# Cross-attention and FFN on one core: heads 0 to 7 of all four tiles first, then heads 8 to 15

## The chip, the core and the metric

One core of one Trainium2 chip. The metric is the device time of one execution in microseconds (us), lower is better; runs are compared by their medians.

## The reference

Eight batches; in each, 512 query rows attend to a context of 1024 rows, then a small FFN with a low-rank term follows. The mask lets through only keys that the kernel finds at run time to lie in a window of 160.

```python
# x [8,512,256], ctx [8,1024,256], 16 heads of 64
def xattn(query, key, value, mask, w_q, w_k, w_v, w_o):
    q, k, v = query @ w_q, key @ w_k, value @ w_v            # 256 -> 1024, split in 16 heads
    scores = jnp.where(mask, -jnp.inf, q @ k.T / 8)          # per head
    return (softmax(scores) @ v).merge_heads @ w_o           # 1024 -> 256
x = x + xattn(layernorm(x), ctx, ctx, mask, ...)
w = clip(round(kernel / s), -8, 7) * s                       # s = max|kernel| / 7
h = layernorm(x)
out = x + h @ w + bias + (h @ a) @ b
```

## The kernel before

**Slots.** A batch has ST = 4 tiles of 128 query rows and NG = 4 groups of 4 heads, so NS = 16 slots per batch; a slot is one tile with one group. LAST = 128 slots in all, and 12 more drain the pipeline (SLOTS, L371). Slot k is tile k % 16 // 4 and group k % 4: a tile goes through all its heads before the next one starts. u is k % 16.

**The pipeline over slots.** Five engines each run through `slot(s)` in order, held together by semaphores only.

- PE (`fast_pe`, `slot`): `scores(k+2)` (L981, 12 matmuls), `weighted_values(k-3)` (L913 with a 65-column output and L1002, 16 matmuls), then the *items* of slot k.
- DVE (`fast_dve`, `slot`, L862 on): normalises the output of slot k-4 (L868, L869), then evacuates the low half of the **first** projection item of slot k-1 (`first = 1`), then `maxima(k+1)` (L801, L805), then the rest of slot k-1's items; in slots 9 to 11 of a batch also the statistics of the layer norm for the batch three ahead (L749, `norm_var`).
- ACT (`fast_act`, `slot`): `exps(k+1)` (L671, 4 instructions), then the high halves of the items of slot k.
- POOL: `split_probs(k)` (L580 to L586) makes fp16 high and low parts of the probabilities; for some slots the per-row 1/sqrt(var) of the tail (L600 to L603).
- SP: a DMA transpose of those parts (L503), residual loads and stores of results.

The scores have two PSUM buffers: `scores(k+2)` waits for `exps(k)`.

**Items.** An item is one PSUM bank's worth of work on PE, whose result ACT rounds to fp16 (high half) and DVE subtracts (low half); matrices are multiplied as three fp16 products (`halves`, L913). Items rotate through three banks (LANES = 3, `p_item`): `claim` makes PE wait until DVE is done with the item three before. Projection items of a batch: c (context transposed), x0, x1 (normalised x transposed), k0 to k3 (keys, four heads each), q0 to q7 (queries, two heads each), v0, v1 (values, eight heads each); once in four batches h, r0, r1 (the rows 129 to 160 of four windows). Tail items of a tile: o0, o1 (attention output transposed, eight heads each), w (the product with w_o and, on DVE, the residual sum x1 and its statistics, L846 to L854), n (x2, the normalised x1, transposed), f (the FFN product and the result, L858). x2 is made on ACT (L716).

**Who is when.** PROJ lists the projection items by u; those of a batch are all made during the batch before it. Batch 0's are all made ahead of slot 0 (ALL_PROJ), and batch 1's by a denser list, FIRST_PROJ. LATE lists the tail items by k % 4, with how many tiles back: every four slots bring one n, one w, one f, one o0 and one o1, w alone in its slot. No projection items remain in batch 7.

```python
PROJ = [["c", "x0"], [], ["x1"], ["k0", "k1"], ["k2", "k3"], [], ["q0"], ["q1"],
        ["q2", "q3"], [], ["q4"], ["q5"], ["q6", "q7"], [], ["v0"], ["v1"]]
LATE = [[("n", 3)], [("w", 2)], [("f", 3), ("o0", 1)], [("o1", 1)]]
```

Of the kernel before, what the change touches and what calls it, by code (L numbers as in the profile page):

```python
# [25 lines left out]
P = 128  # L26
# [11 lines left out]
def xattn_ffn(nc, x, ctx_in, mask, w_q, w_k, w_v, w_o, kern, bias, lora_a, lora_b, out):  # L38
# [8 lines left out]
    PV_BEHIND, HALF_BUFS, TURN_BUFS = 3, 3, 4  # L47
    SCALE = DH ** -0.5
# [11 lines left out]
    with es:  # L60
# [127 lines left out]
        attn = [f.take([HD]) for _ in range(2)]  # L188
        lora_at = Layout()
        lora_at.at = f.at  # L190
        lora = lora_at.take([DT, D])
        oT_hi = f.take([HT, P], fp16)
        oT_lo = f.take([HT, P], fp16)
        x1 = f.take([D])
        x1b = [f.take([D]) for _ in range(2)]
# [150 lines left out]
        def item_evacuation(eng, kind, i, j, src, copy, scale_copy):  # L346
# [6 lines left out]
            if kind == "k":  # L353
# [31 lines left out]
        AHEAD = ["x0", "x1"] + [f"q{i}" for i in range(6)]  # L385
        ALL_PROJ = AHEAD + ["h", "c", "q6", "k0", "q7", "k1", "k2", "k3", "v0", "v1", "r0", "r1"]
        SPLIT = ("o0", "o1", "n")

        def slot_items(k):

            proj = list((FIRST_PROJ if k < NS else PROJ)[k % NS]) if k < LAST - NS else []
            if k % (NS * GROUP) // NS == 2 and k < LAST - GROUP * NS and k % NS in QUAD_ITEMS:
                proj.append(QUAD_ITEMS[k % NS])
            late = [(name, k // NG - back) for name, back in LATE[k % NG] if 0 <= k // NG - back < NT]
            return proj, late
# [8 lines left out]
        class Slot:  # L404


            def __init__(self, k):
                self.k = k
                self.u, self.batch, self.par = k % NS, k // NS, k // NS % 2
                self.t, self.g = self.u // NG, self.u % NG  # L410

                self.proj, self.late = slot_items(k)
                self.norm_ahead = k < LAST - 2 * NS
# [66 lines left out]

        def rest_ready(batch):
# [15 lines left out]
        def fast_sp(sp):  # L497
# [18 lines left out]
            def slot(s):  # L516
                if s.k < LAST:
                    turn_probs(s.k)
                if s.k == 0:
                    sp.wait_ge(keep_made, 1)  # L520
                    sp.wait_ge(zeros_made, 5)
                    rest_values(0)
                if s.u == 4 and s.batch + 1 < B:
                    rest_values(s.batch + 1)
                if s.u == (4 if s.batch == 0 else 1) and s.norm_ahead:

                    sp.wait_ge(xn_made, ST * (s.batch + 2))
                    sp.dma_start(x_in, x_v[s.batch + 2]).then_inc(x_loaded, 16)
                tile = s.k // NG - 1
# [5 lines left out]
                tile = s.k // NG - 3  # L535
                if s.g == 3 and 0 <= tile:
                    sp.wait_ge(out_made, tile + 1)
                    sp.dma_start(outt_v[tile], y[:, tile % 2]).then_inc(out_stored[tile % 2], 16)
# [20 lines left out]
        def fast_pool(pool):  # L559
# [34 lines left out]
            def slot(s):  # L594
                if s.k < LAST:
                    split_probs(s.k)
                tile = s.k // NG - 2
                if s.g == 2 and 0 <= tile < NT:
# [4 lines left out]
                    nc.gpsimd.tensor_tensor(x1b[tile % 2], x1, bias_all[:, :], ALU.add).then_inc(x1b_made, 1)  # L603
                if s.u == 1 and s.norm_ahead:
                    pool.wait_ge(item_made, ALL_PROJ.index("c") + 1 if s.batch == 0 else items_at[s.k - 1 - NS] + 1)
# [18 lines left out]
        def fast_act(act):  # L624

            def item(s, i, name):

                par = 1 - s.par
# [52 lines left out]
            def tail_item(s, i, name):  # L681
# [4 lines left out]
                else:  # L686
                    m = slice(HT // 2 * int(name[1]), HT // 2 * (int(name[1]) + 1))
                    ins = nc.scalar.activation(oT_hi[:, m, :].rearrange("p t q -> p (t q)"), bank[:, :], ACT.Copy)  # L688
# [3 lines left out]
            for i, name in enumerate(ALL_PROJ):  # L692
# [11 lines left out]
                if name == "k3":  # L704
                    exps(1)
                if name in ("v1", "r1"):
# [5 lines left out]
            def slot(s):  # L712
                for name, tile in s.late:
                    if name == "n":
                        act.wait_ge(t_rstd_made, tile + 1)
                        nc.scalar.activation(x2, x1, ACT.Identity, bias=t_shift[:, :], scale=t_rstd[:, :]) \  # L716
                            .then_inc(x2_made, 1)
# [7 lines left out]
                for i, (name, _) in enumerate(s.late):  # L725
                    if name in SPLIT:
                        tail_item(s, len(s.proj) + i, name)
# [6 lines left out]
        def fast_dve(dve):  # L734
# [26 lines left out]
            def item(s, i, name):  # L761

                par = 1 - s.par
# [43 lines left out]
            for i, name in enumerate(ALL_PROJ):  # L807
# [3 lines left out]
                if name == "k1":  # L811
                    maxima(0)
                if name == "k2":
                    maxima(1)
                if name == "v0":
                    maxima(2)
                if name == "r0":
                    maxima(3)
# [6 lines left out]
            def tail_item(s, i, name, tile):  # L825
# [7 lines left out]
                if name[0] == "o":  # L833
                    m = slice(HT // 2 * int(name[1]), HT // 2 * (int(name[1]) + 1))
                    nc.vector.tensor_tensor(oT_lo[:, m, :].rearrange("p t q -> p (t q)"), bank[:, :],  # L835
                                            oT_hi[:, m, :].rearrange("p t q -> p (t q)"), ALU.subtract) \
# [4 lines left out]
                elif name == "w":  # L841

                    dve.wait_ge(res_loaded[tile % 2], 16 * (tile // 2 + 1))
                    if tile >= 1:
                        dve.wait_ge(x1b_made, tile)
                    nc.vector.scalar_tensor_tensor(out=x1, in0=bank[:, 0:D], scalar=1.0 / (WS * WS),  # L846
# [8 lines left out]
                else:  # L855
                    dve.wait_ge(x1b_made, tile + 1)
                    dve.wait_ge(out_stored[tile % 2], 16 * (tile // 2 + 1))
                    nc.vector.tensor_tensor(y[:, tile % 2], bank[:, 0:D], x1b[tile % 2], ALU.add).then_inc(out_made, 1)  # L858
# [3 lines left out]
            def slot(s):  # L862
                k = s.k - PV_BEHIND - 1
                if 0 <= k < LAST:
# [5 lines left out]
                        attn[k // NG % 2][:, k % NG * GROUP * DH:(k % NG + 1) * GROUP * DH]  # L870
# [32 lines left out]
        def fast_pe(pe):  # L903
# [18 lines left out]
            def item(s, i, name):  # L922

                kind, j = name[0], int(name[1:] or 0)
                bank = claim(s, i)
                if kind == "c":
# [31 lines left out]
            def queries_done(batch, grp):  # L958

                last = f"q{2 * grp + 1}"  # L960
                if batch == 0:
                    return max(ALL_PROJ.index(last), ALL_PROJ.index(f"k{grp}")) + 1
                k = next(k for k in range((batch - 1) * NS, batch * NS) if last in slot_items(k)[0])
                return Slot(k).item(slot_items(k)[0].index(last), 1)

            def scores(k):

                par, t, grp = k // NS % 2, k % NS // NG, k % NG
# [18 lines left out]
            def weighted_values(k):  # L987

                par, grp = k // NS % 2, k % NG
# [16 lines left out]
            for i, name in enumerate(ALL_PROJ):  # L1006
# [7 lines left out]
                if name == "k1":  # L1014
                    scores(0)
                if name == "k2":
                    scores(1)
                if name == "v0":
                    scores(2)
                if name == "r0":  # L1020
                    scores(3)
# [3 lines left out]
            def tail_item(s, i, name, tile):  # L1025

                bank = claim(s, i)
                if name[0] == "o":

                    pe.wait_ge(attn_made, NG * tile + (2 if name == "o0" else 4))  # L1030
                    for m in range(HT // 2):
                        c = int(name[1]) * HT // 2 + m
                        mm = nc.tensor.transpose(bank[:, m * P:(m + 1) * P],  # L1033
                                                 attn[tile % 2][:, c * P:(c + 1) * P], ident[:, :])
                elif name == "w":
                    if tile == 0:
                        pe.wait_ge(split_lo[3], 1)
                    pe.wait_ge(item_done, items_at[s.k - 1])
                    mm = halves(bank[:, 0:D], [(oT_hi[:, m, :], oT_lo[:, m, :], wt(3, 0)[:, m, :],
                                                wt(3, 1)[:, m, :]) for m in range(HT)])  # L1040
# [581 lines left out]
```

## Time and profile before

| | us |
|---|---|
| median of 3 runs | 501.69 (500.94 to 502.58) |
| the profiled execution | 500.28 |
| its span, first to last instruction | 497.3 |

The profiled execution lies 3.0 us over its span (what comes before and after the instructions) and 1.4 us under the median. Busy shares of the span are PE 90%, PE weight loads 65%, DVE 81%, ACT 66%, POOL 80%. Such shares are a mean over stretches with different limits, so the views to read are the busy time by batch and the chain of waits within a few slots.

### The profile page before, as it was taken

To read this page: it belongs to the slowest core of one execution; us is meant where nothing else is said; L and a number is where in the kernel's file an instruction comes from. 1 tells how busy PE (TensorE), PEld (TensorE's weight loads), DVE (VectorE), ACT (ScalarE), POOL (GpSimd) and SP (SyncE) were. 2 spreads that over 40 slices of the span, in tenths; PEclk is the share of its full clock that TensorE was granted. 3 is DMA by queue.
4 is the path that set the end of the run, shared out by engine and by line. 5 is a ranking of instruction groups with operands and counts; after the bars stand their busy time and mean duration, and the time that the engine had idled before them with its cause. 6 is when DMAs were issued, how large, how long until landed. Compare 5 with 4: busy or idle time off the path is not lost.

```text
span 497.3 us, 15466 instructions
## 1 busy us (share of the span) xinstructions
PE 448.2 (90%) x5855; PEld 325.1 (65%) x5855; DVE 403.5 (81%) x1110; ACT 327.2 (66%) x845; POOL 398.4 (80%) x659
## 2 busy tenths in 40 slices
PE   3878789999999999999999999999999999888874
PEld 1335556787766866777666866687667876676652
DVE  4876779987988989788988989888988888878662
ACT  4967566875677766776677766776677666656530
POOL 5786578999788977789788978898787977899941
PEclk9789999999999999999999999999999999999897
DMA  8602585797857996789866985799776976779950
GB/s 292 206 23 43 117 192 111 137 201 160 160 115 144 190 153 118 119 181 162 147 125 134 195 160 119 148 171 168 137 132 126 163 153 122 146 139 173 150 127 27
DMA packets 218818, 71.91 MB, mean 145 GB/s; under 512 B 202786, under 2 KB 216883, under 8 KB 218739
## 3 DMA queue, kind: packets, MB, share of 16 engines
q1 hardware_dynamic: 217680, 69.25, 72.7%
q0 software_dynamic: 480, 1.31, 1.0%
q8 instruction: 49, 0.80, 0.7%
q10 hardware_dynamic: 578, 0.30, 0.2%
q14 instruction: 31, 0.25, 0.2%
HBM read 14.71 MB, written 4.19 MB: 38 GB/s over the span
## 4 chain that ended last, share of the span: by engine, by line
PE 42%; DVE 25%; ACT 17%; POOL 8%; issue 4%; DMA 2%; SPq 0%; DVEq 0%; POOLq 0%; ACTq 0%
PE ps_b L913 32%; ACT arena L671 8%; DVE ps_a L801 8%; PE ps_a L981 6%; DVE arena L794 4%; DVE arena L783 2%; ACT arena L650 2%; POOL arena L584 2%; POOL arena L580 2%; DMA arena<-in_L_xattn_w_q_dram 2%; DVE arena L869 2%; ACT arena L662 2%; PE ps_b L1033 2%; ACT arena L622 1%; DVE arena L805 1%
## 5 line engine op out<-in xcount | busy, mean ns | idle before, releaser
L913 PE MATMUL ps_b<-arena 128*128 128x65 f16 (+3 forms) x3348 | 321.6, 248 | 8.3 <-DVE arena L869 4.2
L913 PEld LDWEIGHTS ps_b<-arena 128*128 128x128 f16 x3348 | 222.5, 98 | 84.1 <-issue 7.9
L671 ACT ACTIVATE arena<-ps_a,arena 128x160 f32<-128x160 f32 x512 | 159.9, 395 | 93.5 <-DVE arena L805 84.9
L584 POOL TENSOR_TENSOR arena<-arena 128x512 f16<-128x512 f32 x128 | 148.1, 1157 | 0.0
L580 POOL CAST arena<-arena 128x512 f16<-128x512 f32 x128 | 78.2, 611 | 54.3 <-ACT arena L671 53.3
L801 DVE TENSOR_REDUCE ps_a<-ps_a 128x4 f32<-128x640 f32 x128 | 105.3, 823 | 0.0
L981 PE MATMUL ps_a<-arena 64*128 64x160 f16 x1536 | 75.8, 231 | 13.2 <-ACT arena L671 13.2
L981 PEld LDWEIGHTS ps_a<-arena 64*128 64x128 f16 x1536 | 50.5, 94 | 38.1 <-issue 20.6
L1002 PE MATMUL ps_b<-arena 128*128 128x65 f16 x512 | 71.4, 193 | 0.0
L869 DVE TENSOR_TENSOR arena<-ps_b,arena 128x256 f32<-128x256 f32 x128 | 54.3, 424 | 4.4
L794 DVE TENSOR_TENSOR arena<-ps_b,arena 128x512 f16<-128x512 f32 x60 | 41.1, 687 | 20.2 <-ACT arena L662 18.9
L688 ACT ACTIVATE arena<-ps_b 128x512 f16<-128x512 f32 x64 | 38.4, 602 | 25.6 <-PE ps_b L1033 25.6
L586 POOL TENSOR_TENSOR arena<-arena 128x128 f16<-128x128 f32 x128 | 54.8, 428 | 0.0
L581 POOL CAST arena<-arena 128x256 f16<-128x256 f32 x128 | 51.2, 400 | 0.0
L1002 PEld LDWEIGHTS ps_b<-arena 128*128 128x128 f16 x512 | 50.1, 98 | 0.0
L835 DVE TENSOR_TENSOR arena<-ps_b,arena 128x512 f16<-128x512 f32 x64 | 43.8, 686 | 5.8 <-DVE mask_u L858 1.0
L662 ACT ACTIVATE arena<-ps_b 128x512 f16<-128x512 f32 x58 | 34.9, 604 | 17.7 <-PE ps_b L913 16.5
L1033 PE MATMUL ps_b<-ident,arena 128*128 128x128 f32 x256 | 38.4, 273 | 0.1
L1033 PEld LDWEIGHTS ps_b<-ident,arena 128*128 128x128 f32 x256 | 30.2, 141 | 4.8 <-DVE arena L835 0.2
L600 POOL TENSOR_TENSOR arena<-arena,neg_half 128x1 f32<-128x1 f32 x32 | 17.7, 552 | 17.4 <-DVE arena L854 17.1
L805 DVE TENSOR_SCALAR arena<-ps_a 128x4 f32<-128x4 f32 x128 | 20.7, 162 | 4.4
L868 DVE RECIPROCAL arena<-ps_b 128x4 f32<-128x4 f32 x128 | 22.2, 174 | 2.5 <-PE ps_b L1002 2.1
(139 smaller groups left out, 418.8 us busy)
## 6 DMA issues: line engine op xcount, KB each, us to landing
arena<-in_x_dram SPq DMA_DIRECT2D x8, 512.0 KB
mask_u<-in_x_dram SPq DMA_DIRECT2D x32, 128.0 KB, 2.9
out_dram<-mask_u SPq DMA_DIRECT2D x32, 128.0 KB, 2.6
arena<-arena SPq DMA_TRANSPOSE x128, 4.0
arena<-arena SPq DMA_DIRECT2D x24, 65.0 KB, 2.6
arena<-in_L_xattn_w_q_dram SPq DMA_DIRECT2D x1, 1024.0 KB, 8.7
arena<-in_L_xattn_w_k_dram SPq DMA_DIRECT2D x1, 1024.0 KB, 10.7
arena<-in_L_xattn_w_v_dram SPq DMA_DIRECT2D x1, 1024.0 KB, 12.3
```

What stands on the lines that cost most here:

```text
L580: nc.gpsimd.tensor_copy(hi_main, main).then_inc(p_hi_made, 1)
L581: nc.gpsimd.tensor_copy(rests[:, :, 0:2, :], rest.unsqueeze(2).broadcast_to([P, GROUP, 2, REST])) \
L584: nc.gpsimd.tensor_tensor(lo_main, main, hi_main, ALU.subtract)
L586: nc.gpsimd.tensor_tensor(rests[:, :, 2, :], rest, rests[:, :, 0, :], ALU.subtract).then_inc(p_lo_made, 1)
L671: ins = nc.scalar.activation(probs[k % 2][:, h, :], p_scores[k % 2][:, h % 2, h // 2 * WINDOW:(h // 2 + 1) * WINDOW], ACT.Exp, bias=neg_ma ...
L794: ins = nc.vector.tensor_tensor(f_q[par][:, 1, j, :], bank[:, :], f_q[par][:, 0, j, :], ALU.subtract)
L801: link(nc.vector.tensor_reduce(p_max[k % 2].rearrange("p (i e) -> p e i", e=2), p_scores[k % 2][:, :, 0:2 * WINDOW].rearrange("p e (i k) - ...
L869: nc.vector.tensor_tensor(attn[k // NG % 2][:, k % NG * GROUP * DH:(k % NG + 1) * GROUP * DH] .rearrange("p (h d) -> p h d", h=GROUP), out ...
L913: mm = nc.tensor.matmul(dst, a, c, start=(first and at == 0), stop=(last and at == n - 1))
L981: mm = nc.tensor.matmul(p_scores[k % 2][:, e, i * WINDOW:(i + 1) * WINDOW], f_q[par][own, q_half, m, t * P:(t + 1) * P], f_k[par][own, k_h ...
L1002: mm = nc.tensor.matmul(dst, turn[:, 2, e, :], vr[par][:, h, :], start=False, stop=True)
L1033: mm = nc.tensor.transpose(bank[:, m * P:(m + 1) * P], attn[tile % 2][:, c * P:(c + 1) * P], ident[:, :])
```

## The change

Slot k is now half k % 16 // 8, tile k % 8 // 2 and group 2 * half + k % 2: the four tiles go through heads 0 to 7 in slots 0 to 7, and through heads 8 to 15 in slots 8 to 15. What the second half needs (q4 to q7, k2, k3, v1: OWN) is made in slots 0 to 7 of its own batch; the rest for the next batch is made in slots 6 to 14. So q6, q7, k2, k3 and v1 of batch 0 leave the start, and batch 7 gets seven projection items. Tiles end at slots 9, 11, 13 and 15, so the tail items come every two slots in a part of the batch: tile t's o0 at slot 5 + 2t, its o1 at 13 + 2t, w at 15 + 2t, n at 18 + 2t, f at 20 + 2t (counted on into the next batch). By u the items are now:

| u | items | u | items |
|---|---|---|---|
| 0 | q4 q5 k2 | 8 | x1 n f |
| 1 | w o1 | 9 | c q0 o0 |
| 2 | q6 q7 n | 10 | k0 k1 f |
| 3 | w o1 | 11 | q1 o0 |
| 4 | k3 n f | 12 | q2 (h) |
| 5 | w o0 | 13 | q3 (r0) o1 |
| 6 | x0 n f | 14 | v0 (r1) |
| 7 | v1 o0 | 15 | w o1 |

DVE's w now waits for the x2 of the tile before (`x2_made`), and ACT makes x2 at the end of its slot, one slot ahead of n, instead of at the beginning of n's slot. Each item's own instructions, the scores, the values and their counts stay. The core of the diff (buffers: half-size `attn`, `oT_hi`/`oT_lo` with a part per tile for the first half, three `x1b`):

```diff
-        PROJ = [["c", "x0"], [], ["x1"], ["k0", "k1"],
-                ["k2", "k3"], [], ["q0"], ["q1"],
-                ["q2", "q3"], [], ["q4"], ["q5"],
-                ["q6", "q7"], [], ["v0"], ["v1"]]
-        QUAD_ITEMS = {5: "h", 7: "r0", 11: "r1"}
-        FIRST_PROJ = [["c", "x0"], ["x1"], ["k0", "k1"], ["k2"],
-                      ["k3", "q0"], ["q1"], ["q2"], ["q3", "q4"],
-                      ["q5"], [], ["q6"], ["q7", "v0"],
-                      ["v1"], [], [], []]
+        PROJ = [["q4", "q5", "k2"], [], ["q6", "q7"], [],
+                ["k3"], [], ["x0"], ["v1"],
+                ["x1"], ["c", "q0"], ["k0", "k1"], ["q1"],
+                ["q2"], ["q3"], ["v0"], []]
+        OWN = ("q4", "q5", "q6", "q7", "k2", "k3", "v1")
+        QUAD_ITEMS = {12: "h", 13: "r0", 14: "r1"}
-        LATE = [[("n", 3)], [("w", 2)], [("f", 3), ("o0", 1)], [("o1", 1)]]
+        HALF = NS // 2
+        GH = NG // 2
+        LATE = [("w", 6), ("o1", 4), ("o0", 4 - HALF), ("f", 11), ("n", 9)]
-        ALL_PROJ = AHEAD + ["h", "c", "q6", "k0", "q7", "k1", "k2", "k3", "v0", "v1", "r0", "r1"]
+        ALL_PROJ = AHEAD + ["h", "c", "k0", "k1", "v0", "r0", "r1"]
+        def place(k):
+            half, rest = divmod(k % NS, HALF)
+            return half, rest // GH, half * GH + rest % GH
+        def tile_at(k, after):
+            rest = k - after - (HALF + GH - 1)
+            if rest < 0 or rest % GH or rest % NS >= HALF or rest // NS >= B:
+                return None
+            return rest // NS * ST + rest % NS // GH
         def slot_items(k):
-            proj = list((FIRST_PROJ if k < NS else PROJ)[k % NS]) if k < LAST - NS else []
+            proj = [name for name in PROJ[k % NS] if (k < LAST - NS if name not in OWN else
+                                                      k < LAST and (k >= NS or name not in ALL_PROJ))]
...
-                tile = s.k // NG - 2
-                if s.g == 2 and 0 <= tile < NT:
+                tile = tile_at(s.k, 7)
+                if tile is not None:
                     pool.wait_ge(t_var_made, tile + 1)
...
             def slot(s):
-                for name, tile in s.late:
-                    if name == "n":
-                        act.wait_ge(t_rstd_made, tile + 1)
-                        nc.scalar.activation(x2, x1, ACT.Identity, bias=t_shift[:, :], scale=t_rstd[:, :]) \
-                            .then_inc(x2_made, 1)
                 if DEEP - 1 <= s.k < LAST - 1:
                     exps(s.k + 1)
...
+                tile = tile_at(s.k, 8)
+                if tile is not None:
+                    act.wait_ge(t_rstd_made, tile + 1)
+                    nc.scalar.activation(x2, x1, ACT.Identity, bias=t_shift[:, :], scale=t_rstd[:, :]) \
+                        .then_inc(x2_made, 1)
...
                     if tile >= 1:
                         dve.wait_ge(x1b_made, tile)
+                        dve.wait_ge(x2_made, tile)
...
+                if s.k >= 0 and name in ("q0", "k0"):
+                    pe.wait_ge(item_done, made_at("x1" if name == "q0" else "c", s.batch + 1))
```

## Rows read from the trace of the kernel before

**Rows 1.** Busy time by stretch (us, us busy, clock): batches 0, 2, 4, 7.
```profile
51.76:97.70 45.94, 40.84 (x565) 28.48 (x565) 40.04 (x106) 29.99 (x83) 34.44 (x59) 1.00 0.71 143
...
152.88:210.42 57.54, 56.19 (x742) 41.02 (x742) 49.31 (x136) 39.82 (x107) 46.77 (x80) 1.00 0.81 145
...
265.37:320.16 54.79, 53.22 (x727) 39.66 (x727) 47.44 (x133) 38.19 (x104) 46.71 (x80) 1.00 0.81 152
...
429.49:474.30 44.81, 36.51 (x584) 29.79 (x584) 35.49 (x102) 26.57 (x77) 41.58 (x72) 0.96 0.93 159
```

**Rows 2.** PE by time in batch 4 (start, us, what): u = 1 to 3.
```profile
268.95 0.59 PE L981 MATMUL ps_a<-arena 64*128 64x160 f16 x12 [0.34 <-ACT arena L671]
...
269.97 2.78 PE L913 MATMUL ps_b<-arena 128*128 128x256 f16 x24
272.68 0.59 PE L981 MATMUL ps_a<-arena 64*128 64x160 f16 x12
...
273.70 0.63 PE L939 MATMUL ps_b<-ident,arena 128*128 128x128 f32 x4
274.17 0.82 PE L913 MATMUL ps_b<-arena 128*128 128x256 f16 x6
274.82 0.60 PE L1033 MATMUL ps_b<-ident,arena 128*128 128x128 f32 x4
...
276.37 1.82 PE L913 MATMUL ps_b<-arena 128*128 128x160 f16 x24
```

**Rows 3.** PE by time, batch 0: two query items.
```profile
70.07 2.75 PE L913 MATMUL ps_b<-arena 128*128 128x512 f16 x12
```

**Rows 4.** The chain of waits in batch 0 (start, us, what).
```profile
71.18 1.25 ACT arena L671 x4
72.43 0.50 ACT arena L662
...
72.95 0.69 DVE arena L794
73.64 0.75 DVE ps_a L801
...
74.42 0.17 DVE arena L805
...
74.61 1.26 ACT arena L671 x4
```

**Rows 5.** ACT by time in batch 4: the exponentials of u = 0 to 4, an x2.
```profile
267.56 1.25 ACT L671 ACTIVATE arena<-ps_a,arena 128x160 f32<-128x160 f32 x4 [0.29 <-DVE arena L805]
...
270.79 1.25 ACT L671 ACTIVATE arena<-ps_a,arena 128x160 f32<-128x160 f32 x4 [0.67 <-DVE arena L805]
273.21 1.25 ACT L671 ACTIVATE arena<-ps_a,arena 128x160 f32<-128x160 f32 x4 [1.16 <-DVE arena L805]
...
276.66 1.25 ACT L671 ACTIVATE arena<-ps_a,arena 128x160 f32<-128x160 f32 x4 [0.60 <-DVE arena L805]
...
279.16 0.59 ACT L716 ACTIVATE arena<-arena 128x256 f32<-128x256 f32 x1
279.75 1.25 ACT L671 ACTIVATE arena<-ps_a,arena 128x160 f32<-128x160 f32 x4
```

**Rows 6.** DVE by time in batch 4: item w, and a pair of norm statistics.
```profile
273.13 0.42 DVE L846 SCALAR_TENSOR_TENSOR arena<-ps_b,mask_u 128x256 f32<-128x256 f32 x1
...
274.40 0.17 DVE L868 RECIPROCAL arena<-ps_b 128x4 f32<-128x4 f32 x1
...
297.83 0.74 DVE L749 BATCH_NORM_STATS2 arena<-arena 128x6 f32<-128x256 f32 x2
```

**Rows 7.** The start by time: ACT's exponentials of slot 4.
```profile
56.85 1.25 ACT L671 ACTIVATE arena<-ps_a,arena 128x160 f32<-128x160 f32 x4 [0.43 <-DVE arena L805]
```

**Rows 8.** The end by time: POOL's last two splits, PE's last w (24) and f (6).
```profile
469.10 0.62 POOL L580 CAST arena<-arena 128x512 f16<-128x512 f32 x1
...
474.30 0.61 POOL L580 CAST arena<-arena 128x512 f16<-128x512 f32 x1
...
476.33 0.43 POOL L586 TENSOR_TENSOR arena<-arena 128x128 f16<-128x128 f32 x1
...
484.34 3.44 PE L913 MATMUL ps_b<-arena 128*128 128x256 f16 x30
```

More of the change, by code:

```diff
@@ L187, in xattn_ffn @@
         raw_w = [raw_q, raw_k, raw_v, f_raw.take([DT * HD])]
-        attn = [f.take([HD]) for _ in range(2)]
         lora_at = Layout()
-        lora_at.at = f.at
+        lora_at.at = f.at + HT * D
+        attn = [f.take([HD // 2]) for _ in range(2)]
         lora = lora_at.take([DT, D])
-        oT_hi = f.take([HT, P], fp16)
-        oT_lo = f.take([HT, P], fp16)
+        oT_hi = f.take([ST + 1, HT // 2, P], fp16)
+        oT_lo = f.take([ST + 1, HT // 2, P], fp16)
         x1 = f.take([D])
-        x1b = [f.take([D]) for _ in range(2)]
+        x1b = [f.take([D]) for _ in range(X1B_BUFS)]
         x2 = f.take([D])
@@ L392, in slot_items @@
             if k % (NS * GROUP) // NS == 2 and k < LAST - GROUP * NS and k % NS in QUAD_ITEMS:
                 proj.append(QUAD_ITEMS[k % NS])
-            late = [(name, k // NG - back) for name, back in LATE[k % NG] if 0 <= k // NG - back < NT]
+            late = [(name, tile_at(k, after)) for name, after in LATE if tile_at(k, after) is not None]
             return proj, late
@@ L477, in ffn_weights, with made_at @@
             nc.vector.tensor_tensor(ffn_w[:, :, :], ffn_t[:, :, :], lora, ALU.add).then_inc(ffn_made, 1)
+        def made_at(name, batch):
+            if batch == 0 and name in ALL_PROJ:
+                return ALL_PROJ.index(name) + 1
+            u = next(u for u in range(NS) if name in PROJ[u])
+            k = (batch if name in OWN else batch - 1) * NS + u
+            return items_at[k] + slot_items(k)[0].index(name) + 1
         def rest_ready(batch):
@@ L534, in slot @@
                     sp.dma_start(x_res[:, tile % 2], xt_v[tile]).then_inc(res_loaded[tile % 2], 16)
-                tile = s.k // NG - 3
-                if s.g == 3 and 0 <= tile:
+                tile = tile_at(s.k, 12)
+                if tile is not None:
                     sp.wait_ge(out_made, tile + 1)
@@ L596, in slot @@
                     split_probs(s.k)
-                tile = s.k // NG - 2
-                if s.g == 2 and 0 <= tile < NT:
+                tile = tile_at(s.k, 7)
+                if tile is not None:
                     pool.wait_ge(t_var_made, tile + 1)
@@ L626, in item @@
             def item(s, i, name):
-                par = 1 - s.par
+                par = s.par if name in OWN and s.k >= 0 else 1 - s.par
                 kind, j = name[0], int(name[1:] or 0)
@@ L686, in tail_item @@
                 else:
-                    m = slice(HT // 2 * int(name[1]), HT // 2 * (int(name[1]) + 1))
-                    ins = nc.scalar.activation(oT_hi[:, m, :].rearrange("p t q -> p (t q)"), bank[:, :], ACT.Copy)
+                    part = tile % ST if name == "o0" else ST
+                    ins = nc.scalar.activation(oT_hi[:, part].rearrange("p t q -> p (t q)"), bank[:, :], ACT.Copy)
                 ins.then_inc(item_hi, 1)
@@ L724, in slot @@
                     item(s, i, name)
-                for i, (name, _) in enumerate(s.late):
+                for i, (name, tile) in enumerate(s.late):
                     if name in SPLIT:
-                        tail_item(s, len(s.proj) + i, name)
+                        tail_item(s, len(s.proj) + i, name, tile)
+                tile = tile_at(s.k, 8)
+                if tile is not None:
+                    act.wait_ge(t_rstd_made, tile + 1)
+                    nc.scalar.activation(x2, x1, ACT.Identity, bias=t_shift[:, :], scale=t_rstd[:, :]) \
+                        .then_inc(x2_made, 1)
                 if s.norm_ahead and s.u >= NS - ST:
@@ L761, in item @@
             def item(s, i, name):
-                par = 1 - s.par
+                par = s.par if name in OWN and s.k >= 0 else 1 - s.par
                 kind, j = name[0], int(name[1:] or 0)
@@ L833, in tail_item @@
                 if name[0] == "o":
-                    m = slice(HT // 2 * int(name[1]), HT // 2 * (int(name[1]) + 1))
-                    nc.vector.tensor_tensor(oT_lo[:, m, :].rearrange("p t q -> p (t q)"), bank[:, :],
-                                            oT_hi[:, m, :].rearrange("p t q -> p (t q)"), ALU.subtract) \
+                    part = tile % ST if name == "o0" else ST
+                    nc.vector.tensor_tensor(oT_lo[:, part].rearrange("p t q -> p (t q)"), bank[:, :],
+                                            oT_hi[:, part].rearrange("p t q -> p (t q)"), ALU.subtract) \
                         .then_inc(item_done, 1)
@@ L857, in tail_item @@
                     dve.wait_ge(out_stored[tile % 2], 16 * (tile // 2 + 1))
-                    nc.vector.tensor_tensor(y[:, tile % 2], bank[:, 0:D], x1b[tile % 2], ALU.add).then_inc(out_made, 1)
+                    nc.vector.tensor_tensor(y[:, tile % 2], bank[:, 0:D], x1b[tile % X1B_BUFS], ALU.add).then_inc(out_made, 1)
                     dve.wait_ge(out_made, tile + 1)
@@ L925, in item @@
                 bank = claim(s, i)
+                if s.k >= 0 and name in ("q0", "k0"):
+                    pe.wait_ge(item_done, made_at("x1" if name == "q0" else "c", s.batch + 1))
+                if s.k >= 0 and name == "r0":
+                    pe.wait_ge(item_done, rest_ready(s.batch + 2))
                 if kind == "c":
@@ L958, in queries_done @@
             def queries_done(batch, grp):
[L960 to L964, printed above, removed]
+                return max(made_at(name, batch) for name in (f"q{2 * grp}", f"q{2 * grp + 1}", f"k{grp}"))
             def scores(k):
-                par, t, grp = k // NS % 2, k % NS // NG, k % NG
+                par = k // NS % 2
+                _, t, grp = place(k)
                 if t == 0:
@@ L987, in weighted_values @@
             def weighted_values(k):
-                par, grp = k // NS % 2, k % NG
+                par = k // NS % 2
+                half, t, grp = place(k)
+                if k % HALF == 0:
+                    pe.wait_ge(item_done, made_at(f"v{half}", k // NS))
                 pe.wait_ge(turned[k % TURN_BUFS], 16 * (k // TURN_BUFS + 1))
@@ L1013, in fast_pe @@
                 item(start, i, name)
[L1014 to L1021, printed above, removed]
+                if name in ("k1", "v0", "r0", "r1"):
+                    scores(("k1", "v0", "r0", "r1").index(name))
             pe.wait_ge(keep_made, 1)
@@ L1038, in tail_item @@
                     pe.wait_ge(item_done, items_at[s.k - 1])
-                    mm = halves(bank[:, 0:D], [(oT_hi[:, m, :], oT_lo[:, m, :], wt(3, 0)[:, m, :],
-                                                wt(3, 1)[:, m, :]) for m in range(HT)])
+                    mm = halves(bank[:, 0:D], [(oT_hi[:, part, m], oT_lo[:, part, m], wt(3, 0)[:, c + m, :],
+                                                wt(3, 1)[:, c + m, :])
+                                               for part, c in ((tile % ST, 0), (ST, HT // 2)) for m in range(HT // 2)])
                 elif name == "n":
```

32 lines of the change are left out of this document (13 added, 19 removed).

## The prediction

> **What bounds the kernel now.** I read the busy time by batch first. In a steady batch (batch 4) PE is busy 53.2 of 54.8 us and DVE 47.4, POOL 46.7; batch 2, which carries h, r0 and r1, takes 57.5; batch 0 takes 45.9 for its last 14 slots with PE busy 89% of it, and batch 7, which makes no projections, 44.8 with PE at 81% and POOL at 93% [rows 1]. So the body is filled by PE, and the two ends are not. Batches 1 to 6 run from 97.70 to 429.49, 331.8 us in all.
>
> The second view is PE by time, for the price of an item on PE, from one start to the next. A slot's scores and values take 1.02 (268.95 to 269.97), w 2.71 (269.97 to 272.68), an x of four transposes 0.47, f 0.65, and an o about as much as an x, 0.53; a busy time is 0.16 longer than the step to the next one, so two k are 1.66 and two q 2.59 [rows 2, 3]. v has the form of q, 1.30; n and c are half an x, 0.3. By these prices a batch is 16 x 1.02 and 36.4 of items, 52.8 us.
>
> The third view is the one that decides here, the chain of waits where PE does not fill the time [rows 4]. The exponentials of a slot start at 71.18, those of the next at 74.61, and between them stand, one after the other: exponentials 1.25, ACT's high half of the slot's first projection item 0.5, DVE's low half 0.69, the maximum 0.75 and its scaling 0.17. That is **3.43 us per slot, however little PE has to do**, because DVE evacuates the first projection item ahead of the next maximum, ACT puts the item's high half behind its exponentials, and scores(k+2) waits for exps(k). ACT's starts in batch 4 show the same ring by kind of item: 3.23 after a c (267.56 to 270.79), 2.42 in a slot without a projection item, 3.45 after an x, 3.09 after a k [rows 5]. In the kernel before it rarely stops PE, since projection slots (3.43 at most) alternate with w slots, where PE needs 3.73 and the ring 2.42 or less.
>
> **The change, part by part.** It adds no matmul. It moves items, and so the question is which slots get shorter than the ring.
>
> *Heavy slots, u = 15 and 0 to 5.* Four of w and o at 1.02 + 2.71 + 0.53 = 4.26; q4 q5 k2 4.45; q6 q7 n 3.92; k3 n f 2.80. Together 28.2 us, all PE's, as the ring needs at most 3.43 here.
>
> *Light slots, u = 6 to 14.* Each has a projection item first, nine in a row. PE's work is 9 x 1.02 + 15.4 = 24.6 us. The ring from the exponentials of slot 6 to those of slot 14 needs 3 x 3.43 for x0, v1 and x1, 3.23 for c, 3.09 for k0 and 3 x 3.43 for q1 to q3, 26.9. Before it, the exponentials of slot 6 come 1.1 after PE enters the slot: ACT must first make the o0 of slot 5 and the x2 that is now behind it, each about 0.6 [rows 5], less an overlap. After it, scores follow exponentials by 1.3 to 1.4 (267.56 to 268.95) [rows 2, 5]. So slots 6 to 14 take 1.1 + 26.9 + 1.3 = 29.3 instead of 24.6. A batch is 28.2 + 29.3 = 57.5.
>
> *Waits that are new in this order.* In slots 4 and 6 there are three items behind a [w, o] slot, and f needs the bank of that o. DVE's w now waits for the x2 before it, which stands on ACT behind the o: about 1.2 into the slot, then w for 1.27 (273.13 to 274.40), then o for 0.6: f can start at 3.1, and PE's work before it is 2.15 in slot 4, so +0.9 there [rows 6]. In slot 6 the same delay goes into the ring, because DVE reaches x0 late: +0.8. In slots 9 to 11 DVE does norm statistics (0.74 a pair) [rows 6] beside two or three items per slot: its own work from one maximum to the next is then 3.4, 3.8 and 3.6 by the durations above, against 3.2, 3.1 and 3.4 of the ring, +1.1. Queued behind these waits on DVE are the next maximum, behind it ACT's exponentials and PE's scores. I take all three, 2.8, so a batch is **60.2 us**; with none of them 57.5, and below that only as rival 2 has it. POOL has 46.7 per batch [rows 1] and its tail work every second slot falls where slots last 4.3, so I cost it at nothing; if that cover were gone the bound is its wait for w's statistics, again DVE's.
>
> *Batches 1 to 6.* Five at 60.2; batch 6, which prepares no norm, 59.1; and h, r0, r1 in slots 12 to 14, where PE waits anyway, cost 1.0 instead of the 2.7 of before (57.5 against 54.8) [rows 1]. 361.1 against 331.8: +29.3.
>
> *The start.* q6, q7, k2, k3 and v1 leave it: 3 x 1.30 + 2 x 0.83 = 5.6 us of PE, on the path, since the start is one chain through PE, ACT and DVE. The exponentials of slot 4 stood at 56.85 [rows 7]; I walk them to 52. From there slots 4 and 5 and DVE's FFN preparation are 9.2, the ring from 6 to 14 26.9 and 0.7 for the statistics, then 1.3 and slot 15 with 4.26: batch 1 starts at 94.4 instead of 97.70, **-3.3**. Batch 0 gives back 2.3 of the 5.6, since its light slots are bound by the ring too.
>
> *The end.* Batch 7 begins with the same heavy slots, now with its own q4 to q7, k2, k3: 24.8 us for slots 0 to 5 (28.2 less slot 15, and the 0.9 of slot 4). By the same walk POOL is done with the last of four tails 4.1 later; it then has nine splits at 2.4 (474.30 to 476.76) [rows 8] with 0.7 lost at v1: its last split ends 51.1 after the batch's start, before 476.7 - 429.5 = 47.2, +3.9. Behind it three w instead of two still lie around and after the last values: one more w in line (2.7), the new wait of w for x2 and the o behind it (1.8), and 0.7 of waiting for the x2 of tile 28. The last w ended 57.6 after the batch's start (484.34 + 2.7) [rows 8], now 66.7; what follows it is unchanged. **+9.1** with the 3.9.
>
> Sum: -3.3 + 29.3 + 9.1 = +35.1 on a span of 497.3, that is 532.4, and 535.4 for the profiled execution of 500.28. Against the median of 501.69, 1.4 higher, it is **536.8 us**.
>
> The Trainium skill, "Perfetto Trace Analysis", section "Optimization Strategy", says that a kernel whose limiting engine changes over time may gain from interleaving those regimes. This change does the reverse inside a batch: w slots and projection slots alternated and now stand in two blocks. The rule gives no figure, and the sum above does without it.
>
> **The rivals.**
>
> *1. The ring is hidden, and PE's work alone counts.* Then a batch is 52.8 instead of 54.8 to 55.3, since the stall of slot 0 (265.37 to 268.95, 3.58 against 2.1 of work) [rows 1, 2] goes too: 6 x -2.4 = -14, -3.3 to -5.6 at the start, +5 at the end for eight more us of PE in a batch with about 8 us of PE idle: 488 us. For it: PE is busy 97% of a batch. Against it: 3.43 in rows 4 with PE waiting. 6%.
>
> *2. The ring holds, but the boundary swallows most of it.* If the exponentials of slot 6 come 1.0 before PE enters the slot, as is possible once ACT is not held by o and x2, the light slots 6 to 14 are 27.2 and a batch 55.4, as before. What is left is -3.3 and +5: 503; with half of the difference 515. Against it: the o is PE's last item of slot 5, so ACT cannot be early. 14%, of which 3% lie within 0.3% of before.
>
> *3. Slower, and more: the clock falls in the light slots.* PE would be idle 20% of slots 6 to 14. Batch 7 had PE at 81% and a granted clock of 0.96, batch 0 89% and 1.00 [rows 1]. At 1.2 GHz for slots 12 to 14 their 7.4 us of PE work become 14.8, against 10.3 of the ring, +4.5 in each of seven batches: 536.8 + 31 = 568. 7%. The Trainium skill, "TensorE: Matmul & The Clock Gate", section "A second HAM failure mode: psum-queue depth-cycling", describes a kernel whose short idle times between matmul groups that cycle through PSUM banks made the clock swing; by that rule this rival would be the likely one, and batch 7, with much the same idle share at 0.96, speaks against it.
>
> *The forecast*, ring and DVE waits as walked, 522 to 550: 73%.
>
> **How the numbers follow.** The time is the forecast's, 536.8. Its own range is from no new waits (57.5 per batch: 6 x -2.7 = -16, 521) to 1.5 us more per batch and 4 at the end (550). The range for 8 in 10 adds the upper half of rival 2: 512 to 552. A difference of 0.3%, 1.5 us, is about what a measurement of this kernel can tell from none. Faster: rival 1 and a part of 2, 0.07; same: 0.03; slower: 0.90.
>
> **What would show it.** In the profile after: PE's busy share in batches 1 to 6 falls from 97% to about 88%; PE's scores wait for ACT's exponentials in u = 7 to 15; exponentials stand 3.4 us apart in u = 6 to 14 while slots 15, 1, 3 and 5 take 4.3; DVE's w waits for x2; batch 1 starts near 94; the last split of POOL ends some 51 us after batch 7 began. Wrong would be: exponentials closer than 3.2 in the light slots (the ring is not a ring), a batch under 57 (rival 2), a clock under 0.97 in the body (rival 3), or a start that gains nothing.

## The result

The changed kernel takes **548.65 us** (median of 4 runs, 544.81 to 550.84) against 502.01 (4 runs) for the kernel before: ratio 1.0934, 95% interval 1.0878 to 1.0991. It is slower, by 46.6 us; forecast were 536.8 and 512 to 552. The profiled execution took 544.81 with a span of 543.0. One of the four runs of e6 below is in the chip's slower state (553.47 at a granted clock of 0.944), so its time is given as the median of the other three.

Busy time by batch, changed kernel, as rows 1 had it for the kernel before (stretch, its length, then us busy of PE, PE's weight loads, DVE, ACT and POOL, granted clock): the last 14 slots of batch 0, batches 1, 4 and 6, batch 7 up to the end of POOL's last split, the end.

```profile
48.42:99.00 50.58, 38.61 (x519) 26.52 (x520) 39.02 (x96) 30.67 (x85) 36.42 (x61) 0.93 0.75 136
...
99.00:159.39 60.39, 54.31 (x728) 39.61 (x728) 47.30 (x133) 37.68 (x103) 47.93 (x81) 1.00 0.76 140
...
281.32:341.71 60.39, 54.30 (x727) 39.59 (x727) 47.38 (x133) 37.68 (x103) 46.84 (x80) 1.00 0.72 138
...
402.10:462.10 60.00, 54.24 (x727) 39.59 (x727) 45.58 (x122) 36.33 (x100) 44.68 (x77) 1.00 0.70 128
462.10:513.20 51.10, 43.07 (x625) 32.81 (x625) 37.84 (x107) 29.53 (x83) 43.51 (x75) 0.97 0.78 138
513.20:543.00 29.80, 16.69 (x177) 13.88 (x174) 11.52 (x41) 5.50 (x11) 5.81 (x13) 0.95 0.22 56
```

A steady batch is 60.39 us instead of 54.79 [rows 1], with the same instructions on every engine: DVE is busy for 47.4, POOL for 46.8. PE was busy 97% of a batch and is now busy 90%. The chain of waits through slots 5 to 8 of batch 4 (start, us, what) says why (whole lines are left out at the dots):

```profile
302.98 2.62 PE ps_b L927 x24
305.60 0.45 PE ps_b L1045 x4
...
306.57 0.60 ACT arena L745
...
307.29 0.44 DVE arena L860
307.75 0.43 DVE arena L864
...
308.64 0.60 DVE arena L848
309.24 0.10 DVE arena L882
309.37 0.42 DVE arena L883
309.79 0.60 DVE arena L793
310.39 0.75 DVE ps_a L820
311.16 0.17 DVE arena L824
311.36 1.25 ACT arena L690 x4
312.61 0.59 ACT arena L669
313.22 0.75 DVE arena L802
313.98 0.75 DVE ps_a L820
314.75 0.17 DVE arena L824
314.94 1.12 ACT arena L690 x4
```

Read it downwards: PE's w and o of slot 5 end the heavy stretch (L927, L1045). ACT makes x2 behind the o (L745). DVE's w waits for that x2 (L860); then come its o (L848), the output of an older slot (L882, L883), x0's low half (L793) and the maximum (L820). From 311.36 on it is the ring of the prediction, that is, the closed round of waits from one slot's exponentials to the next slot's: exponentials, v1's high half (L669) and low half (L802), maximum, exponentials at 314.94, 3.58 later. PE is in none of the lines after 306. The waits by sum over the whole execution (who waited for whom: us in all, times, longest) show the same two places. The second line did not exist before, and PE's wait for the exponentials grew from 13.2 to 30.7 us:

```profile
ACT arena L690 <- DVE arena L824: 96.5, 88, 2.4
...
DVE arena L860 <- ACT arena L745: 48.0, 23, 3.7
PE ps_a L996 <- ACT arena L690: 30.7, 39, 2.9
```

### The profile page after: what moved, and what is told of

The parts are those of the page before. It is cut to its first block, busy times and chain, and to the rows that moved or that the text cites. A ratio compares the mean times of both kernels' runs of the same rounds, so it can differ in the third digit from the quotient of the medians.

```text
span 543.0 us, 15520 instructions
## 1 busy us (share of the span) xinstructions
PE 454.8 (84%) x5855; PEld 326.7 (60%) x5855; DVE 405.4 (75%) x1110; ACT 324.6 (60%) x845; POOL 399.3 (74%) x659
## 4 chain that ended last, share of the span: by engine, by line
PE 40%; DVE 36%; ACT 15%; issue 5%; DMA 2%; POOL 1%; SPq 0%; DVEq 0%
PE ps_b L927 31%; ACT arena L690 9%; DVE ps_a L820 8%; PE ps_a L996 5%; DVE arena L813 3%; DVE arena L848 3%; PE ps_b L1045 3%; DVE arena L883 2%; ACT arena L745 2%; DVE arena L824 2%; DVE arena L793 2%; DVE arena L860 1%; DVE arena L864 1%; DVE arena L768 1%; ACT arena L681 1%
## 5 line engine op out<-in xcount | busy, mean ns | idle before, releaser
L927 PE MATMUL ps_b<-arena 128*128 128x65 f16 (+3 forms) x3348 | 326.2, 249 | 22.2 <-DVE arena L883 5.7
L927 PEld LDWEIGHTS ps_b<-arena 128*128 128x128 f16 x3348 | 223.4, 98 | 97.9 <-issue 11.4
L820 DVE TENSOR_REDUCE ps_a<-ps_a 128x4 f32<-128x640 f32 x128 | 105.3, 823 | 0.0
L996 PE MATMUL ps_a<-arena 64*128 64x160 f16 x1536 | 76.2, 232 | 31.4 <-ACT arena L690 30.7
L996 PEld LDWEIGHTS ps_a<-arena 64*128 64x128 f16 x1536 | 51.0, 95 | 59.9 <-ACT arena L690 29.8
L883 DVE TENSOR_TENSOR arena<-ps_b,arena 128x256 f32<-128x256 f32 x128 | 54.3, 424 | 4.4
L860 DVE SCALAR_TENSOR_TENSOR arena<-ps_b,mask_u 128x256 f32<-128x256 f32 x32 | 13.6, 424 | 54.6 <-ACT arena L745 48.0
L848 DVE TENSOR_TENSOR arena<-ps_b,arena 128x512 f16<-128x512 f32 x64 | 43.6, 681 | 0.0
L1045 PE MATMUL ps_b<-ident,arena 128*128 128x128 f32 x256 | 38.5, 273 | 0.0
L1045 PEld LDWEIGHTS ps_b<-ident,arena 128*128 128x128 f32 x256 | 30.7, 141 | 5.9 <-DVEq L874 0.9
L882 DVE RECIPROCAL arena<-ps_b 128x4 f32<-128x4 f32 x128 | 22.2, 174 | 4.8 <-PE ps_b L1020 4.3
```

The source lines that it names most:

```text
L820: link(nc.vector.tensor_reduce(p_max[k % 2].rearrange("p (i e) -> p e i", e=2), p_scores[k % 2][:, :, 0:2 * WINDOW].rearrange("p e (i k) - ...
L848: nc.vector.tensor_tensor(oT_lo[:, part].rearrange("p t q -> p (t q)"), bank[:, :], oT_hi[:, part].rearrange("p t q -> p (t q)"), ALU.subt ...
L883: nc.vector.tensor_tensor(attn[k // GH % 2][:, k % GH * GROUP * DH:(k % GH + 1) * GROUP * DH] .rearrange("p (h d) -> p h d", h=GROUP), out ...
L927: mm = nc.tensor.matmul(dst, a, c, start=(first and at == 0), stop=(last and at == n - 1))
L996: mm = nc.tensor.matmul(p_scores[k % 2][:, e, i * WINDOW:(i + 1) * WINDOW], f_q[par][own, q_half, m, t * P:(t + 1) * P], f_k[par][own, k_h ...
L1045: mm = nc.tensor.transpose(bank[:, m * P:(m + 1) * P], attn[pair % 2][:, m * P:(m + 1) * P], ident[:, :])
```

## The experiments

**e1 to e4: the two causes, one at a time and together.** e1 and e2 turn DVE's order in the changed kernel and in the kernel before:

```diff
-                first = 1        # low half of the slot's first projection item, then maxima
+                first = 0        # maxima first
```

e3 makes x2 on ACT earlier, behind the exponentials of its slot and ahead of the slot's high halves; e4 is both on the changed kernel.

```diff
                 if DEEP - 1 <= s.k < LAST - 1:
                     exps(s.k + 1)
+                tile = tile_at(s.k, 8)
+                if tile is not None:
+                    act.wait_ge(t_rstd_made, tile + 1)
+                    nc.scalar.activation(x2, x1, ACT.Identity, bias=t_shift[:, :], scale=t_rstd[:, :]) \
+                        .then_inc(x2_made, 1)
...
                         tail_item(s, len(s.proj) + i, name, tile)
-                tile = tile_at(s.k, 8)
-                if tile is not None:
-                    act.wait_ge(t_rstd_made, tile + 1)
-                    nc.scalar.activation(x2, x1, ACT.Identity, bias=t_shift[:, :], scale=t_rstd[:, :]) \
-                        .then_inc(x2_made, 1)
```

> The changed kernel with DVE's order turned: the maximum of a slot ahead of the first projection item, so that the item's high and low half leave the ring of exponentials, high half, low half, maximum. Theory (the ring sets slots 6 to 14): exponentials no longer stand 3.4 us apart there, slots 11 to 14 shrink to PE's 2.4 to 2.9, a steady batch falls from 60.4 to 55 to 57 us, and the whole to about 515 us. Rival (banks, DVE's load or the DMA transposes hold the light slots): a batch stays within 1 us of 60.4 and the time within 1% of 548.65.

> The kernel before with the same turn of DVE's order. Theory: the ring binds here only in batch 0 (14 slots in 45.9 us) and in the slot behind v1 (3.58 instead of 2.1), so batch 0 falls by 2 to 4 us, a steady batch from 54.8 to 53 to 54, and the whole to 490 to 495 us. Rival (the order of maxima matters nowhere): 501.7 within 0.3%.

> The changed kernel with x2 made on ACT right behind the exponentials of its slot instead of behind the high halves of that slot's items, so that DVE's w doesn't wait for the o that PE makes after it. Theory: slot 4 loses 0.9, slot 6 1.2, the exponentials behind w slots come 0.5 earlier, and a steady batch is 2 to 3 us shorter (57.5 to 58.4); the whole about 530 us, 3 of it at the end. Rival (DVE's wait for x2 costs nothing, since the ring follows anyway): a batch stays within 0.5 us of 60.4.

> The changed kernel with both edits: maximum ahead of the first projection item, and x2 right behind the exponentials. Theory: what is left is PE's work, 52.8 us a batch, plus waits for banks; a batch of 53 to 55, the whole 497 to 507 us. Rival (a third cause in the new order, such as POOL or the DMA transposes): a batch over 57.

Measured, beside 499.9 us for the kernel before on the same chip (13 runs):

| | median us | ratio, 95% interval | steady batch us |
|---|---|---|---|
| e1 maximum first | 527.47 | 1.0556 (1.0503 to 1.0608) | 57.88 |
| e3 x2 early | 530.38 | 1.0612 (1.0575 to 1.0649) | 58.63 |
| e4 both | 497.99 | 0.9951 (0.9921 to 0.9980) | 54.36 |
| e2 maximum first, kernel before | 489.91 | 0.9817 (0.9796 to 0.9838) | 53.76 |

The rows of batch 4 in e1, e2, e3 and e4 (columns as above):

```profile
270.76:328.64 57.88, 54.70 (x727) 39.92 (x727) 47.31 (x133) 37.83 (x103) 46.51 (x80) 1.00 0.81 147
```
```profile
259.25:313.01 53.76, 52.99 (x727) 39.62 (x727) 47.37 (x133) 37.61 (x104) 46.70 (x80) 1.00 0.83 155
```
```profile
275.06:333.69 58.63, 53.84 (x728) 39.71 (x728) 47.69 (x133) 37.79 (x103) 46.97 (x80) 1.00 0.74 142
```
```profile
258.04:312.40 54.36, 53.68 (x729) 39.94 (x728) 47.35 (x133) 37.84 (x103) 46.66 (x80) 1.00 0.87 155
```

No work was taken away in any of them. Two changes of order, one on DVE and one on ACT, give back 6.0 us a batch (60.39 to 54.36), more than the 5.6 by which it had become longer. The ring is real: in e1 the exponentials that ACT starts in its slots 12 to 15 stand 2.7, 2.6 and 2.5 apart, where they stood 3.4, 3.4 and 3.6:

```profile
317.79 1.25 ACT L690 ACTIVATE arena<-ps_a,arena 128x160 f32<-128x160 f32 x4 [0.43 <-DVE arena L824]
320.47 1.25 ACT L690 ACTIVATE arena<-ps_a,arena 128x160 f32<-128x160 f32 x4 [0.27 <-DVE arena L824]
323.08 1.25 ACT L690 ACTIVATE arena<-ps_a,arena 128x160 f32<-128x160 f32 x4
325.54 1.24 ACT L690 ACTIVATE arena<-ps_a,arena 128x160 f32<-128x160 f32 x4
```

But e1 alone is worth 2.5 us a batch and not the 3.4 to 5.4 expected, and the whole came to 527.5 and not to about 515. The edit has a price of its own: an item's low half now comes one maximum later, and its bank with it. In slot 3 of e1 the w waits for the bank of q6, and slots 3 and 5 take 4.66 instead of 4.17:

```profile
284.88 2.79 PE L927 MATMUL ps_b<-arena 128*128 128x256 f16 x24 [0.32 <-DVE arena L813]
```

With x2 early (e4) slots 3 and 5 are back at 4.17: turning the order is worth 58.63 - 54.36 = 4.3 us on top of e3, and 2.5 without it. x2 early is worth 1.8 alone and 3.5 on top of e1. So each cause hides a part of the other; that this is because both act through DVE's order is my reading. e3 came out near its expectation (530 forecast and 530.4 measured, but 58.6 a batch, just over 57.5 to 58.4), e4 within it (497 to 507, a batch within 53 to 55). e2 is 1.8% **faster than the kernel before** and the fastest of all, at the low edge of its expectation (490 to 495). It gains 3.0 us in batch 0 and 1.0 in a steady batch: slot 0 takes 3.10 instead of 3.58, and slot 12, which the expectation had not named, 3.92 instead of 4.45. With both changes of order the new grouping is 0.5% under the kernel before (e4), and e2, the old grouping with one of them, is 1.6% below that again: regrouping by itself bought nothing.

**e5: the changed kernel again.**

> The changed kernel once more, for its time beside the kernel before on one chip and for a second trace of it. Theory: a steady batch of 60.4 us again, the ratio within 1.085 to 1.10. Executions differed by 1% with the granted clock (0.957 to 0.982); if the clock falls where PE waits for the ring, the low digits stand in the light slots or in the start, not in the heavy slots.

547.89 us, ratio 1.0992 (1.0931 to 1.1053), beside 500.07 for the kernel before. Batches 1, 3 and 4 again took 60.4, but batches 5 and 6 took 61.7 and 61.6. The difference comes from one slot of each, slot 9, which lasted 6.07 and 5.97 instead of 4.42 (in batch 5 slot 12 gives 0.4 of it back). In the first of them PE by time:

```profile
374.52 0.44 PE L1057 MATMUL ps_b<-ident,arena 128*128 128x128 f32 x2 [0.59 <-DVE arena L848]
375.21 0.59 PE L996 MATMUL ps_a<-arena 64*128 64x160 f16 x12 [0.24 <-ACT arena L690]
...
376.42 0.44 PE L948 MATMUL ps_b<-ident,arena 128*128 128x128 f32 x2
377.78 2.74 PE L927 MATMUL ps_b<-arena 128*128 128x512 f16 x6 [0.93 <-DVEq L874]
```
```profile
375.21:377.50 2.29, 1.61 (x30) 1.12 (x30) 1.79 (x4) 0.87 (x3) 2.29 (x4) 1.00 0.94 179
377.50:381.28 3.78, 3.50 (x10) 1.62 (x11) 3.08 (x10) 2.24 (x8) 2.61 (x5) 0.55 0.66 141
```

q0 takes 2.74 us for its six matmuls; in the changed kernel's first trace the same six took 1.47. The granted clock of the stretch is 0.55, TensorE's lower level of 1.2 GHz for most of it, behind three waits of PE (0.59, 0.24, 0.93) within 5 us. Batch 4 of the same trace has the same waits in slot 9 and keeps a clock of 1.00 there. The same slot, and no other in batches 1 to 6, was long in batches 2, 4, 5 and 6 of the traces of e6 and e7 below, by about 1.5 us each, and batches 1 to 6 together took 367.8 and 368.0 us there against 363.1 in the first trace. So the 1% by which executions of the changed kernel differ is made, in part at least, of this: 0 to 4 slots at half clock. The expectation (light slots, not heavy ones) held, but the waits of slot 9 are for banks more than for the ring. The Trainium skill, "TensorE: Matmul & The Clock Gate", section "A second HAM failure mode: psum-queue depth-cycling", describes clock swings from short idle times between matmul groups that cycle through PSUM banks; this agrees, though only in one slot of sixteen and not in every batch.

**e6: the start as before.** ALL_PROJ is the old list, so batch 0's q6, q7, k2, k3 and v1 are made ahead of slot 0.

> The changed kernel with q6, q7, k2, k3 and v1 of batch 0 made ahead of slot 0 as in the kernel before (for batch 0 alone). Theory (what leaves the start was hidden there under the chain through ACT and DVE, and kept TensorE's clock up): batch 1 starts within 1.5 us of the changed kernel's 99.0, so the move gained nothing. Rival (the start was bound by PE's work, as the prediction had it): batch 1 starts 2 to 5 us later, and the whole is that much longer.

547.26 us, ratio 1.0913 (1.0858 to 1.0968): no difference that can be told from the changed kernel. For the start itself the traces must be laid on one another at the same instruction, because the setup before it varies by over 1 us; one of DVE's setup that all have, in the kernel before and in the changed kernel:

```profile
29.25 0.15 DVE L1535 CAST flag<-span 128x1 int32<-128x1 f32 x1
```
```profile
30.55 0.15 DVE L1548 CAST flag<-span 128x1 int32<-128x1 f32 x1
```

From there to the start of batch 1 it is 97.70 - 29.25 = 68.45 us before and 99.00 - 30.55 = 68.45 after; in e5 68.5, in e6 67.4. **Taking five items out of the start gained nothing**, and putting them back costs nothing: batch 1 even starts 1.0 sooner. (By the raw times it starts at 96.6, 2.4 before the changed kernel's 99.0 and outside the 1.5 of the expectation; the rival's 2 to 5 us later is out either way.)

PE itself does arrive sooner: it enters slot 2 17.9 us behind that instruction instead of 22.5. But the exponentials before it are 3.6 apart as before (3.58, 3.59 and 3.58; before 3.07, 3.59 and 3.58), and the chain of waits has no line of PE from 38 to 58.7 us, in either trace. Between two exponentials it reads, in the changed kernel:

```profile
47.41 0.96 ACT arena L690 x3
48.37 0.59 ACT arena L677
...
48.98 0.75 DVE arena L808
49.73 0.75 DVE ps_a L820
...
50.50 0.17 DVE arena L824
...
50.70 1.25 ACT arena L690 x4
```

It is the ring again. The exponentials that stood at 56.85 [rows 7] are at 56.06, 25.5 behind that instruction instead of 27.6. Those 2.1 us are given back by the end of batch 0, whose light slots are bound by the ring (42.9 from there to batch 1 instead of 40.9).

The clock of the start is lower than before, 0.93 from that instruction to batch 1 against 0.98. In PE's rows k0 and k1 (24 matmuls, 3.23 us; the like of them took 1.82 in rows 2) and q6 and q7 (12 in 4.10; 2.75 in rows 3) run slowly, in stretches with a granted clock of 0.80 and 0.65:

```profile
34.75 3.23 PE L927 MATMUL ps_b<-arena 128*128 128x160 f16 x24 [1.43 <-DVE arena L787]
...
49.23 4.10 PE L927 MATMUL ps_b<-arena 128*128 128x512 f16 x12
```

But the items that left are not shown to be what kept the clock up: the first stretch had 0.81 in the kernel before, with them, and e6, where they are back, has 0.87 over the whole start.

**e7: batch 7 without its own seven items.** `k < LAST` becomes `k < LAST - NS` for OWN, and the scores and values of batch 7's second half use what older batches left.

> The changed kernel without the seven projection items of batch 7's second half (q4 to q7, k2, k3, v1 are left out there; older values are used in their place). Theory: of the 13 us that the end takes longer, these items hold 4 to 6, so 538 to 541 us by the profile's 544.8; the rest is the crowding of the tails, three w and four x2 behind the last values, and stays. Rival (the items of batch 7 carry nearly all of it): 10 us or more less.

550.03 us, ratio 1.0994 (1.0956 to 1.1032): no gain, against both expectations. Batch 7 up to the last split and the end, as above:

```profile
467.04:516.10 49.06, 38.38 (x568) 30.26 (x568) 34.20 (x100) 25.92 (x76) 43.51 (x75) 0.88 0.80 146
516.10:549.50 33.40, 19.31 (x179) 15.29 (x177) 11.52 (x41) 5.50 (x11) 5.75 (x13) 0.91 0.19 47
```

Batch 7 is only 2.0 us shorter up to the last split (51.1 to 49.1), not 4 to 6. Slots 0, 2 and 4, where most of the items were, are 5.5 shorter together, but slots 3 and 5 are 3.6 longer (6.70 and 5.21 instead of 4.17 each). In slot 3 the clock fell to 0.75, and its w took 3.89 instead of 2.78.

Behind the last split e7 took 33.4 instead of 29.8. That can't be put down to the edit, because in e6's trace the items of batch 7 are all there and its end is long too (from the start of batch 7 to the end of the span):

```profile
464.39:549.20 84.81, 63.91 (x799) 49.26 (x798) 49.41 (x148) 35.07 (x94) 49.33 (x87) 0.92 0.57 103
```

With the same instructions in batch 7 and behind it, this stretch took 80.9 in the first trace (clock 0.96), 81.0 in e5 and 84.8 in e6; e7's 82.5 (clock 0.89) lies between. So e7 shows that leaving the items out doesn't bring back the 13.1 us by which this stretch had grown (67.8 before), but not how many they hold, nor how much of the end is the tails' crowding and how much the clock. That the x2 wait is 3.5 of it is shown by e3 (452.2 to 529.6 is 77.4, the changed kernel 462.1 to 543.0 is 80.9).

**e8: the light slots spread anew.** On e4: `["x1"], ["c"], ["q0"], ["q1"], ["k0", "k1", "q2"], ["q3"], ["v0"]` for slots 8 to 14, h in slot 10.

> e4 (maximum first, x2 early) with the light slots' items spread anew: c alone in slot 9, q0 in 10, q1 in 11, k0 k1 q2 in 12, h in 10. Theory: what is left above PE's work in e4's batch of 54.4 are waits for banks in slots 9 to 11 (3.66, 3.64 and 3.20 us against 3.13, 3.33 and 2.83 of work), so a batch is 53.2 to 54.0 and the whole 3 to 6 us under e4's 498.0. Rival (no such wait, or the three items of slot 12 bring it back): within 1 us of e4.

503.16 us, ratio 1.0062 (1.0034 to 1.0090); a batch is 55.09, 0.7 longer than e4's, and the whole 5 us longer, so both the theory and the rival (within 1 us of e4) missed. Slot 12 with its three items takes 4.61 us for 3.98 of work, and slot 10 3.74 for 2.95. Neither waits for a bank. In both PE's values wait for DVE's normalisation of an older output (L883), 0.63 in slot 10 and 0.34 in slot 12:

```profile
298.80 0.25 PE L927 MATMUL ps_b<-arena 128*128 128x65 f16 x3 [0.63 <-DVE arena L883]
```

On DVE that output stands behind the norm's work for a later batch: a pair of statistics before slot 10's, the variances (L775 to L778) before slot 12's. In batch 6, which prepares no norm, slots 10 and 12 take 3.09 and 4.07, and the batch 53.65, as e4's batch 6 (53.57). So the new order costs its 0.7 us only where the norm's work stands beside it.

## Why the prediction was right

*The ring, right in kind and size.* Slots 6 to 14 were to take 29.3 + 0.8 + 1.1 = 31.2 us and took 31.57 in batch 4 (305.97 to 337.54); the heavy slots 0 to 5 24.8 and took 24.65; slot 15 4.26 and took 4.17. A batch was to be 60.2 and is 60.39. e1, e2 and e4 changed the ring by an order alone and the time went with it.

*The new waits, right as a sum, one mis-sized.* The x2 wait was to cost 0.9 in slot 4 and 0.8 in slot 6; without it (e3) a batch is 1.8 shorter, slot 4 2.82 instead of 3.70. The norm statistics were to cost 1.1, but batch 6, which prepares no norm, is only 0.4 shorter (60.00 against 60.39). The prediction had no wait for banks in the light slots, and there is one: in slot 9 q0 waits 0.93 for the bank of f, which DVE empties only behind x1's low half and the maximum, and the slot takes 4.42 in batch 6 too. The exponentials that ACT starts in its slots 9 to 12 are 3.41, 3.86 and 3.64 apart in batch 4 and 3.24, 3.07 and 4.21 in batch 6: the statistics do cost the ring 1.0 in the first two, but in batch 6 most of that is lost again in the third. That the sum of the light slots came out within 0.4 is in part luck.

*Batches 1 to 6:* 361.1 forecast, 363.1 measured (99.00 to 462.10), of which 0.9 in batch 6. h, r0 and r1 cost 1.15 (batch 2, 61.54), forecast 1.0.

*The start: the step that failed.* -3.3 was forecast and the gain is 0.0; the step was "5.6 us of PE, on the path". PE wasn't on the path there: the exponentials of slots 0 to 3 hang on the same ring of ACT and DVE, which I had found in batch 0 and didn't carry back into the start. The exponentials of slot 4 were walked to 52 and stood at 56.06; the walk from there to batch 1 was right, 42.4 forecast and 42.9 measured. With 1.3 us by which this trace's setup was later, that is 4.6 of the 9.4 us between 535.4 and the profiled 544.8.

*The end: right up to the last split, short behind it.* The last split ends 51.1 us after batch 7 begins, as forecast. What follows was to be 25.8 and is 29.8. I had the new wait for x2 and the o behind it once; DVE's w waits for x2 twice here, 3.63 and 3.73 us:

```profile
514.59 0.42 DVE L860 SCALAR_TENSOR_TENSOR arena<-ps_b,mask_u 128x256 f32<-128x256 f32 x1 [2.91 <-PE ps_b L927]
...
522.19 0.42 DVE L860 SCALAR_TENSOR_TENSOR arena<-ps_b,mask_u 128x256 f32<-128x256 f32 x1 [3.63 <-ACT arena L745]
...
528.76 0.42 DVE L860 SCALAR_TENSOR_TENSOR arena<-ps_b,mask_u 128x256 f32<-128x256 f32 x1 [3.73 <-ACT arena L745]
...
533.67 0.42 DVE L860 SCALAR_TENSOR_TENSOR arena<-ps_b,mask_u 128x256 f32<-128x256 f32 x1 [2.06 <-PE ps_b L927]
```

Four w on DVE, 7.6, 6.6 and 4.9 us apart. In the first two gaps w, o, x2 and the next w stand in a line; the last w waits for PE.

*Sum for the profiled execution:* start 4.6, body 2.0, end 4.0 more than forecast, and 1.2 less around the span (1.8 instead of 3.0): 535.4 + 9.4 = 544.8. The median lies another 3.8 higher, and the other three runs had a clock of 0.957 to 0.966 instead of 0.982. The forecast's own step from the profiled time to the median was 1.4, so 9.4 + 3.8 - 1.4 is the 11.8 between 536.8 and 548.65.

*The rivals.* PE's work alone (1) and a boundary that swallows the ring (2) are out by the traces. The falling clock (3) is partly true: not in slots 12 to 14 and not for 4.5 us in every batch, but for about 1.5 us in slot 9 of up to four batches, and in the start and the end.

## What to carry to other kernels

Engines that run through the same slots in a fixed order form rings: follow one from an instruction to its successor in the next slot and sum it, because that sum is the shortest slot, whatever the busiest engine does. Here a kernel with PE at 97% stood just over such a ring (e2: it cost 1.0 us a batch) because heavy slots alternated with light ones; with the work regrouped into heavy and light blocks the ring was paid in full. And the cheapest cure was an order: the maximum ahead of an evacuation that is needed less soon gave the kernel before 1.8%, without a change of work. The order has a price where PE waits for the bank of that evacuation, as e1 showed. And before time at the end or in the start is put down to an edit, look at the same stretch in another trace where it is unedited: here two of them differed by 3.9 us.

## What the runs showed of the hardware

In e5 slot 9, with PE idle for 0.59, 0.24 and 0.93 us in it or just before it, went on at a granted clock of 0.55 in batch 5 and 0.54 in batch 6, and at 1.00 in batch 4, with the same instructions at the same distances. So the clock fell behind waits of which none reached 1 us, but not each time. Six matmuls of 512 columns took 2.74 us at the lower level and 1.47 at the higher one. Where e7 took items from PE around slot 3 of batch 7, that slot ran at a clock of 0.75 and took 6.70 us instead of 4.17. The same instructions of batch 7 and the end took 80.9 us at a clock of 0.96 in one trace and 84.8 at 0.92 in another.
